# A stack of four graph layers: layer 2's projection and bias moved from behind its neighbour sums to ahead of them

## The reference

```
deg_isqrt = max(number of incoming edges, 1) ** -0.5
h = relu(layernorm(x))
y = deg_isqrt[:, None] * (h @ W.T + b)
x = x + deg_isqrt[:, None] * segment_sum(y[src], dst)
```

## Time and profile before

| what | us |
|---|---|
| median of 3 timed runs (lowest, highest) | 3631.68 (3629.55, 3637.06) |
| the profiled execution, its own time | 3632.91 |
| its span, first to last instruction | 3631.1 |
| ACT busy | 850.1 |
| POOL busy | 794.5 |
| steps of passes 0 to 5 on PE (L1085) | 855.9 to 1763.6 |

### The profile page before, as it was taken

One profiled execution on the slowest core, in us unless ns is written; L12 is line 12 of the kernel. 1 busy time (PEld: TensorE's weight loads), 2 busy tenths in 40 slices (PEclk: granted clock), 3 DMA queues, 4 the chain that ended last, 5 costly groups with the idle time before them and its releaser, 6 DMA issues.

```text
span 3631.1 us, 34205 instructions
## 1 busy us (share of the span) xinstructions
PE 3303.6 (91%) x12605; PEld 1842.2 (51%) x12605; DVE 2295.8 (63%) x3020; ACT 850.1 (23%) x1116; POOL 794.5 (22%) x651
## 2 busy tenths in 40 slices
PE   6679985988999999999739999999999999997998
PEld 4567764754544554545514444444444444474444
DVE  9963321344020120535798888888888898877987
ACT  1113331343000001322112222222222222252222
POOL 7888888820000000000101111111111000010000
PEclk6569997998999999999869999999999999998999
DMA  9999997992434344222456556555655432284422
GB/s 325 364 330 284 307 273 175 281 243 81 145 117 142 120 132 154 78 71 68 129 164 165 113 121 147 118 132 118 138 116 130 106 94 73 77 294 128 122 67 66
DMA packets 278001, 572.57 MB, mean 158 GB/s; under 512 B 92265, under 2 KB 156246, under 8 KB 275787
## 3 DMA queue, kind: packets, MB, share of 16 engines
q1 hardware_dynamic: 140795, 432.89, 37.5%
q0 software_dynamic: 84560, 77.50, 13.1%
q10 hardware_dynamic: 52480, 60.01, 5.6%
HBM read 365.44 MB, written 204.86 MB: 157 GB/s over the span
## 4 chain that ended last, share of the span: by engine, by line
PE 41%; DVE 7%; issue 5%; DMA 2%; ACT 1%; POOL 0%; DVEq 0%; ACTq 0%; POOLq 0%
PE ps L1246 28%; PE ps L1085 3%; PE ps L1210 3%; PE ps L1274 2%; PE ps L1253 2%; DVE R L2173 2%; DMA den_d<-R 1%; DVE wB L2136 1%; DVE PT L1968 1%; DVE wA L1968 1%; PE ps L1038 1%; DVE Fb L1968 1%; PE ps L1276 0%; DVE PT L2136 0%; PE ps L1186 0%
## 5 line engine op out<-in xcount | busy, mean ns | idle before, releaser
L1246 PE MATMUL ps<-R,B 125*128 125x500 f32 x2800 | 1093.9, 542 | 32.9 <-DVE R L2173 26.8
L1246 PEld LDWEIGHTS ps<-R,B 125*128 125x128 f32 x2800 | 503.8, 190 | 595.8 <-issue 552.5
L751 POOL DMA_INDIRECT pairs<-w x392 | 606.6, 1548 | 130.8 <-issue 107.1
L1085 PE MATMUL ps<-R,H 125*128 125x500 f32 (+1 forms) x1400 | 542.6, 542 | 15.1 <-ACT H L1357 7.6
L1484 ACT ACTIVATE R<-R,asc 125x1625 f32<-125x1625 f32 (+1 forms) x200 | 320.2, 1601 | 989.7 <-DVE R L2160 989.7
L2160 DVE SCALAR_TENSOR_TENSOR R<-H,asc 125x1625 f32<-125x1625 f32 (+1 forms) x200 | 368.9, 1845 | 144.7 <-PE ps L1253 113.4
L2173 DVE SCALAR_TENSOR_TENSOR R<-R 125x1625 f32<-125x1625 f32 (+1 forms) x250 | 444.8, 1779 | 0.0
L1085 PEld LDWEIGHTS ps<-R,H 125*128 125x128 f32 x1400 | 253.3, 191 | 283.5 <-issue 280.5
L938 PE MATMUL ps<-R,H 125*128 125x375 f32 (+1 forms) x1000 | 300.4, 447 | 49.3 <-DMA R<-pairs 48.8
L1246 PE MATMUL ps<-R,H 125*128 125x500 f32 (+1 forms) x700 | 274.0, 547 | 19.8 <-DVE R L2173 18.1
L781 POOL DMA_DIRECT2D den_d<-R x138 | 117.4, 851 | 794.6 <-DVE R L2173 770.7
(11 more groups left out here) (319 smaller groups left out, 2948.8 us busy)
## 6 DMA issues: line engine op xcount, KB each, us to landing
pairs<-R SPq DMA_DIRECT2D x25, 3200.0 KB, 18.1
R<-ct_d SPq DMA_DIRECT2D x162, 406.2 KB, 3.5
R<-pairs SPq DMA_DIRECT2D x25, 2500.0 KB, 11.3
R<-ct_d SPq DMA_DIRECT2D x162, 375.0 KB, 3.2
R<-wt_d SPq DMA_DIRECT2D x50, 812.5 KB, 4.4
R<-wt_d SPq DMA_DIRECT2D x50, 750.0 KB, 4.1
den_d<-R POOLq DMA_DIRECT2D x75, 312.5 KB, 5.6
den_d<-R POOLq DMA_DIRECT2D x75, 250.0 KB, 4.8
```

Source lines behind the costliest of these rows:

```text
L751: pool.indirect_dma_start(pairs, bass.IndirectOffsetOnAxis(ap=key_u[:, c:c + 1], axis=0), val[:, c, :], None, compute_op=ALU.add)\
L1085: last = mm(ps[:, bank, at:at + w], rows[0:Q, j, f * 128:(f + 1) * 128], TL[q % TS][0:Q, o:o + w], start=j == 0 and at == 0, stop=j == NB ...
L1246: last = mm(ps[:, bank, at:at + w], rows[0:Q, j, f * 128:(f + 1) * 128], TT[q % TR][0:Q, o:o + w], start=j == 0 and at == 0, stop=j == NB ...
```

## The change

Each source block of layer 2 is now projected before it is summed. Two new items per pair of source blocks stand in `AUX`: `turned` transposes the normalised rows of two blocks (four transposes to bank 7, copied by DVE into `ZT`, which takes the place of weights that are no longer used), and `weighted` multiplies them by `w2T`; DVE adds `norm * b` and writes the rows back into `H`, which the steps read. Pairs of the first 13 blocks use the slots 10 to 23 of pass 3, those of the last 12 the slots 10 to 21 of pass 4. A step of layer 2 waits for `z_ready` where it waited for `ln_done`. The sums then come out finished, and an `out` item of layer 2 only transposes them back, two transposes a block. The count sums `cn` go, with all waits on `cn_made`; `count_tile` keeps the diagonal alone. The item `norms` moves from slot 10 to slot 9 of pass 4.

```diff
--- before.py
+++ after.py
@@ -185,7 +185,6 @@
         C16 = [R[:, 2 * LW + s * HW:2 * LW + (s + 1) * HW].bitcast(U16) for s in range(CS)]
         TL = [R[:, 2 * N + s * LW:2 * N + (s + 1) * LW] for s in range(TS)]
         f2T = Fb[:, 0:2 * LW].rearrange("p (k c) -> p k c", k=KT)
-        cn = [Fb[:, s * LW:(s + 1) * LW] for s in range(2)]
         tmp = [PT[:, s * 2 * D:(s + 1) * 2 * D] for s in range(2)]
         pjunk = PT[:, 4 * D:4 * D + 4 * Q]
 
@@ -200,6 +199,7 @@
 
         wA = sb("wA", [128, 5 * KT * D])
         w01, w02, w11 = [wA[:, k * KT * D:(k + 1) * KT * D].rearrange("p (k n) -> p k n", k=KT) for k in range(3)]
+        ZT = [wA[:, s * KT * D:s * KT * D + 2 * KT * Q] for s in range(2)]
         w12 = wA[:, 3 * KT * D:5 * KT * D].rearrange("p (k n) -> p k n", k=2 * KT)
         wB = sb("wB", [128, 4 * KT * D])
         wl1 = wB[:, 0:2 * KT * D].rearrange("p (k n) -> p k n", k=2 * KT)
@@ -351,12 +351,17 @@
                 AUX.append((it, k))
                 PLAN[k + 1][min(at, NB - 1)].append(len(AUX) - 1)
                 at += 1
+            if k == 3:
+                AUX.append(("norms", None))
+                PLAN[4][9].append(len(AUX) - 1)
+            if k in (2, 3):
+                for n, (b0, nb) in enumerate(PAIRS_OF[k - 2]):
+                    for i, step in enumerate(("turned", "weighted")):
+                        AUX.append(((step, HALF[k - 2][0] + b0, nb), None))
+                        PLAN[k + 1][10 + 2 * n + i].append(len(AUX) - 1)
             if k == 1:
                 AUX.append(("rootr2", None))
                 PLAN[2][at].append(len(AUX) - 1)
-            if k == 3:
-                AUX.append(("norms", None))
-                PLAN[4][10].append(len(AUX) - 1)
             if k == 4:
                 for n, (g_, kk) in enumerate([(g_, kk) for g_ in range(3) for kk in range(KT)] + [(3, KT)]):
                     AUX.append((("turn", g_, kk), None))
@@ -599,7 +604,6 @@
                     uv_rows(p + 2, p // 2 + 1, p % 2, 0)
 
             sp.wait_ge(S("l12_pe"), 6 * NB)
-            sp.wait_ge(S("cn_made"), 2 * NB)
             for r in range(LCR):
                 lc_load(r, *LATE[r])
             for r in range(LCR, len(LATE)):
@@ -1004,6 +1008,20 @@
                         for m in range(nj):
                             last = tr(ps[:, 7, (n * nj + m) * Q:(n * nj + m + 1) * Q], Bn[0:Q, j0 + m, f * 128:(f + 1) * 128],
                                       ident[0:Q, 0:Q])
+                elif it[0] == "turned":
+                    j0, nj = it[1], it[2]
+                    pe.wait_ge(S("ln_done"), 2 * NB + j0 + nj)
+                    for m in range(nj):
+                        for f in range(KT):
+                            last = tr(ps[:, 7, (m * KT + f) * Q:(m * KT + f + 1) * Q],
+                                      H[0:Q, j0 + m, f * 128:(f + 1) * 128], ident[0:Q, 0:Q])
+                elif it[0] == "weighted":
+                    nj = it[2]
+                    for m in range(nj):
+                        for f in range(KT):
+                            at = (m * KT + f) * Q
+                            last = mm(ps[0:Q, 7, m * D:(m + 1) * D], ZT[it[1] // 2 % 2][:, at:at + Q], w2T[:, f, :],
+                                      start=f == 0, stop=f == KT - 1)
                 elif it == "rootr1" or it == "rootr2":
                     pe.wait_ge(S("rootb"), 1 if it == "rootr1" else 2)
                     w = w12 if it == "rootr1" else wl1
@@ -1021,7 +1039,7 @@
                 else:
                     b0, nb = it[1], it[2]
                     layer, h = divmod(k, 2)
-                    src_, w = ((f2T, w12), (aggL, wl1), (aggL, w2T))[layer]
+                    src_, w = ((f2T, w12), (aggL, wl1), (aggL, None))[layer]
                     if layer == 0:
                         c = b0 // 4
                         pe.wait_ge(S("f2_done"), MID[(k, c, KT - 1)] + 1)
@@ -1031,15 +1049,15 @@
                     else:
                         pe.wait_ge(S("evA"), EVA[k + 1])
                         pe.wait_ge(S("evD"), EVD[k + 1])
-                        pe.wait_ge(S("cn_made"), (k - 3) * NB)
                     for m in range(nb):
                         b = b0 + m
                         for f in range(KT):
-                            last = mm(ps[0:Q, 7, m * D:(m + 1) * D], src_[:, f, b * Q:(b + 1) * Q], w[:, f, :],
-                                      start=f == 0, stop=f == KT - 1 and layer < 2)
-                        if layer == 2:
-                            last = mm(ps[0:Q, 7, m * D:(m + 1) * D], cn[h][0:Q, b * Q:(b + 1) * Q], bcs[0:Q, 3, :],
-                                      start=False, stop=True)
+                            if layer < 2:
+                                last = mm(ps[0:Q, 7, m * D:(m + 1) * D], src_[:, f, b * Q:(b + 1) * Q], w[:, f, :],
+                                          start=f == 0, stop=f == KT - 1)
+                            else:
+                                last = tr(ps[0:Q, 7, m * D + f * 128:m * D + (f + 1) * 128],
+                                          aggL[:, f, b * Q:(b + 1) * Q], ident[:, :])
                 last.then_inc(S("aux_pe"), 1)
 
             def early_scores(g):
@@ -1065,7 +1083,7 @@
                 elif layer == 1:
                     pe.wait_ge(S("bn_ready"), j + 1)
                 else:
-                    pe.wait_ge(S("ln_done"), 2 * NB + j + 1)
+                    pe.wait_ge(S("z_ready"), j + 1)
                 if layer < 2:
                     pe.wait_ge(S(f"t_in{q % TS}"), 16 * (q // TS + 1))
                 else:
@@ -1459,8 +1477,6 @@
                 w = COLS[k % 2]
                 act.wait_ge(S(f"c16_in{n % CS}"), 16 * (n // CS + 1))
                 act.wait_ge(S("l12_pe"), q - TS + 1)
-                if n >= TS:
-                    act.wait_ge(S("cn_made"), n - TS + 1)
                 a(TL[q % TS][0:Q, 0:w], C16[n % CS][0:Q, 0:w], ACT.Copy).then_inc(S("cast"), 1)
                 if j == 2:
                     evac_f0(k - 1)
@@ -1816,6 +1832,17 @@
                             .then_inc(S("aux_dve"), 1)
                     else:
                         cp(FE[:, it[2], 0:nj * Q], ps[:, 7, 0:nj * Q]).then_inc(S("aux_dve"), 1)
+                elif it[0] == "turned":
+                    nj = it[2]
+                    cp(ZT[it[1] // 2 % 2][:, 0:nj * KT * Q], ps[:, 7, 0:nj * KT * Q]).then_inc(S("aux_dve"), 1)
+                elif it[0] == "weighted":
+                    for m in range(it[2]):
+                        j = it[1] + m
+                        link.mark(stt(H[0:Q, j, :], bcs[0:Q, 3, :], norm[0:Q, j:j + 1], ps[0:Q, 7, m * D:(m + 1) * D],
+                                      ALU.mult, ALU.add))
+                    link.join()
+                    dve.sem_inc(S("aux_dve"), 1)
+                    dve.sem_inc(S("z_ready"), it[2])
                 elif it == "root1":
                     root_row(ps[:, 7, 0:KT], True)
                     dve.sem_inc(S("aux_dve"), 1)
@@ -1894,22 +1921,13 @@
 
             def count_tile(q):
 
-                n = q - 4 * NB
                 k, j = divmod(q, NB)
-                h, w = k % 2, COLS[k % 2]
-                j0, nj = HALF[h]
-                dve.wait_ge(S("cast"), n + 1)
-                t = TL[q % TS][0:Q, 0:w]
-                if j0 <= j < j0 + nj:
-                    dg = t[:, (j - j0) * Q:(j - j0 + 1) * Q]
-                    tt(dg, dg, ident[0:Q, 0:Q], ALU.subtract).then_inc(S("minus"), 1)
-                    dve.wait_ge(S("minus"), j + 1)
-                c = cn[h][0:Q, 0:w]
-                if j == 0:
-                    ts(c, t, norm[0:Q, j:j + 1], None, ALU.mult).then_inc(S("cn_made"), 1)
-                else:
-                    dve.wait_ge(S("cn_made"), n)
-                    stt(c, t, norm[0:Q, j:j + 1], c, ALU.mult, ALU.add).then_inc(S("cn_made"), 1)
+                j0, nj = HALF[k % 2]
+                if not j0 <= j < j0 + nj:
+                    return
+                dve.wait_ge(S("cast"), q - 4 * NB + 1)
+                dg = TL[q % TS][0:Q, (j - j0) * Q:(j - j0 + 1) * Q]
+                tt(dg, dg, ident[0:Q, 0:Q], ALU.subtract).then_inc(S("minus"), 1)
 
             def attention_columns():
                 dve.wait_ge(S("w31_in"), 16)
```

## The result

The changed kernel is **slower by 0.22%**: the ratio of its times to those of the kernel before is 1.0022, 95% interval [1.0013, 1.0031], that is +8.0 us (4.7 to 11.3) on 18 runs of each. One run of each took about twice as long (6879.66 and 7478.72 us) and doesn't count in the ratio. The median is 3639.66 us beside 3631.07. The forecast was +6.0 us and 3637.7 us: the +6.0 lies in the interval. The middle of the interval lies just outside the 0.2% that I called no change, the interval on both sides of it, so on which side of that border the change falls isn't settled by these runs.

What follows compares the result with a forecast made beforehand. TensorE was taken to bound layer 2's stage, with PE and DVE alternating in the tail. Stage +11.2 and tail -5.2 gave +6.0 us, 3637.7 us against the timed median (0.17% slower); 8-in-10 range 3631 to 3645 us.

Steps and rivals of the forecast that it cites:

- Products and turning, +29.8 - 16.8 us: Layer 2 stage on PE: products 21.6, turning in 5.4 and back 2.8 us added; 13 blocks' old instructions, 16.8, removed.
- Norms, -1.8 us: Pass 4: the norms' small products, moved to slot 9, fill PE's wait for a late cast, gaining 1.8 us.
- The counts at nothing: Layer 2 stage: removing 89 us of count operations from DVE was costed at nothing.
- New waits, 0: Steps waiting for `z_ready` and `turned` for normalised rows: taken as 0, ends -0.5 and +4 us.
- The rival that it binds: `z_ready` binds at many steps, up to 1 us for each of 25 blocks; within 0.03 left to everything else.
- The changes of pass unchanged: Changes of pass in layer 2: PE's waits of 2.4, 2.2 and 0.7 us would still be there.
- +11.2: The stage, first step after 1317 us to last step's end: predicted growth in us, from 446.3 to about 457.5.
- The tail, -5.2 us: Last step's end to last addition: DVE begins 3.3 us earlier and loses 1.9 us idle; 27.0 us becomes 21.8.
- The Trainium skill's rule on transposes: Tail: by it transposes would stay at 1.2 GHz, at no cost if DVE covers them, 2.2 us if uncovered.
- Behind the tail, 0: After the last addition: all should be as before, only 6 us later.
- the first rival: Tail gives nothing back, DVE waiting for the maxima's ring loads instead of PE: +11.2 us, 3642.9 us; chance 0.20.

Runs made afterwards that it cites:

- a_half: Changed kernel with each `weighted` product projecting only the first 128 features, 2 instructions a block instead of 4; ratio to before 0.9992.
- a_norms10: Changed kernel with the `norms` item put back in slot 10 of pass 4; one time, 3640.12 us.
- b_norms9: Kernel before with only the `norms` item moved from slot 10 to slot 9 of pass 4; one time, 3631.64 us.
- b_no_counts: Kernel before with the counts of source blocks 1 to 24 added up over the first 125 columns only; ratio to before 1.0000.
- a_swap_lean: a_swap with the maxima spread anew: 18 in pass 5 instead of 11, none in the tail, the last 8 behind it; ratio to before 0.9979.
- a_swap: Changed kernel with ACT emptying its banks ahead of its third cast and DVE a step earlier; ratio to before 1.0014.
- b_swap_n9_lean: Kernel before with norms in slot 9, banks emptied ahead of the third cast, and a_swap_lean's spread of maxima; ratio to before 0.9991.
- b_best: Kernel before with norms in slot 9, banks emptied ahead of the third cast, two more maxima in pass 5, five in the tail, eight behind; ratio 0.9976.

## Why the prediction was right, and where it was short

- **Products and turning, +29.8 - 16.8 us.** Right. Pass 3 grew by 14.04 us for 14.0 worked out; 0.216 a product and 0.11 a transpose held, and a_half shows that nothing covers them.
- **Norms, -1.8 us.** Right, and short by the 0.2 us that a wait costs beyond its idle time: a_norms10 gives the wait back. It is worth less when the clock falls behind them (b_norms9).
- **The counts at nothing.** Right, by b_no_counts.
- **New waits, 0.** Right: none names `z_ready`'s additions. The rival that it binds falls.
- **The changes of pass unchanged.** Right for the waits (2.4, 2.2, 0.8), short for what follows them. I had costed a wait at its length; with the clock that can fall behind it, it costs 1.7 us more. That was +3.4 us in both profiles of the changed kernel, more than the whole 3.1 us that the stage lay above +11.2. I read the clock of 1.00 in the earlier trace rows as a property of the place, while it was that of one execution.
- **The tail, -5.2 us: mis-sized, by 1.1 in these two profiles.** The mechanism held, DVE is the bound. The first addition came 0.71 us after the first transpose and not 1.26, since the four ran at the full clock (0.67 us): 3.9 us saved for 3.3. Each cycle took 3.42 us for the 3.51 forecast: an addition that needn't wait starts 0.09 us ahead of the recorded end of the maximum, which the idle time in the earlier trace rows doesn't hold. Here too I took the clock of one execution for that of the place: both my sum and the 6.3 us measured start from a tail of 26.97 us at the lower clock. From a tail at the full clock, 25.3 us, the changed tail of 20.68 saves 4.6, so that -5.2 lies between the two and its closeness is in part luck.
- **The Trainium skill's rule on transposes.** In the tail after, the granted clock stands at 0.50 and four transposes take 1.22 us where the first four took 0.67:

```profile
1780.00:1795.00 15.00, 4.86 (x16) 3.67 (x16) 14.28 (x24) 0.00 (x0) 2.69 (x5) 0.50 0.48 154
```

The Trainium skill, "TensorE: Matmul & The Clock Gate", Part 4: PE-mode transpose, states that transposes don't count as PE being busy in the way that matmuls do. The time came out as if by it, and with products in the same place the clock was 1.00, but with products PE was also busy for three quarters of the time and here for a third. Another place in the trace of before speaks against the rule. Behind a standstill of 3.88 us PE makes nothing but transposes; these stretches (columns as in the earlier trace rows) hold no other work of PE:

```profile
834.50:837.50 3.00, 2.98 (x14) 2.98 (x15) 1.69 (x4) 3.00 (x5) 0.00 (x0) 0.50 0.00 0
837.50:838.50 1.00, 1.00 (x9) 1.00 (x9) 0.97 (x3) 1.00 (x2) 0.00 (x0) 0.79 0.00 0
838.50:844.00 5.50, 3.08 (x22) 2.40 (x20) 5.36 (x13) 3.80 (x8) 0.00 (x0) 1.00 0.00 0
846.00:850.00 4.00, 1.99 (x7) 1.41 (x6) 3.90 (x10) 0.00 (x0) 0.00 (x0) 0.50 0.00 0
```

A run of transposes without a gap was followed by a rise from 0.50 to 1.00, and the fall came again once they stood apart, with PE busy for half of the time. So page and measurement differ here, and the measurement decides: transposes as such don't keep the clock low. That it is the idle time between them that does so in the tail is likely and not shown; no run changed the idle time there at the same kind of work enough to tell. As forecast, the low clock cost nothing while DVE covered it; in a_swap_lean it costs 0.47 us in each of the cycles but the first.
- **Behind the tail, 0.** It was +0.5 in both profiles of the changed kernel, in DVE's waits for loads of the ring (1.25 us where before had 0.64): a tenth of what the first rival asked for. In a_swap it was -0.2 and in a_half +0.9, so I don't put it down to the change.

In the profiles the misses are +3.4 (two falls of the clock) and -0.3 in the stage, -1.1 in the tail and +0.5 behind it: +8.5 where +6.0 was forecast. Of the -1.1 in the tail more than the whole is the fall in the tail of before. That the falls of the clock make up +3.4 and 1.7 of this is shown in the traces, by the granted clock and the unchanged instructions; how often each comes in timed runs stays open, and with it whether the true change is nearer +6 or +8 us.

## What to carry to other kernels

Cost each microsecond on the engine that is full, and nothing on the one that isn't, until something waits for it: 70 us of VectorE were worth nothing, 11 us of TensorE cost 11. Room that is won on the second engine becomes time only if work that stands bare elsewhere is moved into it, as a_swap_lean did. A wait of 2 us on TensorE can cost almost twice its length (2.36 us of idle time and 1.7 behind it), so read the granted clock behind each, and in more than one execution of both kernels: here falls of the clock made one side 3.4 us longer and the other 1.7, beside a change of some 7 us.

## What was unexpected of the hardware

- Behind waits of 2.36 us PE's clock fell to 1.2 GHz in 7 of 9 profiles, behind 2.2 us in 2 of 9, behind 2.1 to 2.2 us ahead of the tail's products in 3 of 7, behind 1.8 us in 0 of 5, behind 0.8 to 0.9 us in 0 of 10. A full fall cost 1.7 us. In two executions of one kernel it came once at the first place and once at the tail.
- The clock also fell with no wait at all, behind the norms, 20 products of one or four columns in 2.2 us: in b_norms9, b_swap_n9_lean and b_best, but in none of the six other profiles with the norms in slot 9: 3 of 4 with the projection behind the sums, 0 of 5 with it ahead. The norms end at 1525.6 in b_best:

```profile
1524.00:1527.00 3.00, 3.00 (x17) 2.23 (x17) 2.13 (x3) 3.00 (x3) 0.00 (x0) 0.74 0.35 94
1527.00:1530.00 3.00, 3.00 (x8) 1.33 (x7) 2.93 (x6) 0.70 (x1) 0.00 (x0) 0.69 0.84 235
```

PE was busy for the whole of both stretches and still was granted 0.74 and 0.69 of full speed. What of it the small products cause was not tried.
- The clock can rise while PE makes nothing but transposes: 0.50 from 834.5 to 837.5 us and 1.00 from 838.5 in the trace of before, behind a standstill and in a run of them without a gap.
